# A two-layer perceiver kernel on one core: the second layer's context attention takes its value tiles as 128 keys by 512 columns, in halves, from a bank of their own

## Chip, core and metric

The kernel runs on one core of a Trainium2 chip. The metric is the device time of one execution in microseconds (us), the median of several. The engines are named as in the profile: PE is TensorE's matrix array, PEld its weight loads, DVE is VectorE, ACT is ScalarE, POOL is GpSimd, SP is SyncE, whose queue issues most transfers.

## What is computed

Two layers, each of a context attention, a self attention and a feed-forward part, over x of 8 batches by 128 rows by 512, with a context of 8 by 2048 keys by 512. All numbers are 4-byte floats. The change lies in the second layer's context attention and in the preparation for it:

```python
def _L1_xattn_ref(query, key, value, Wq, bq, Wk, bk, Wv, bv, Wo, bo):   # key = value = ctx_1024, 16 heads of 32
    ...
    q = query @ Wq.T + bq
    k = key @ Wk.T + bk
    v = value @ Wv.T + bv
    ...
    scores = jnp.einsum('bhtd,bhsd->bhts', q, k) * scale
    attn = jax.nn.softmax(scores, axis=-1)
    ctx = jnp.einsum('bhts,bhsd->bhtd', attn, v)
    return ctx @ Wo.T + bo
...
```

## The kernel before

The stages follow one another: the first layer's context attention ("swishmax"), its self attention ("twin"), the self attention of its feed-forward part ("plain"), the experts, then the second layer's context attention ("context", the function softmax_context), its kernel attention ("features") and the last nets. Within a stage each engine has an order of its own, written out by hand as a list of named tiles, and semaphores join them.

The context of a batch is four chunks of 512 keys. The heads are taken in four groups (slabs) of four heads, 128 columns of the weights each. A unit u is one batch b and one slab g (u = 4b + g, 32 in all); a step n is one unit and one chunk c (n = 4u + c). In step n TensorE makes, in the order of pe_step: the scores of (u, c) for four heads, the keys of (u+1, c), in chunk 0 the spread of the row maxima of u-1, in chunk 1 the sums of u-2, the transposed scores of (u-1, c), the values of the next unit, and "attend" of step n-5. VectorE takes the row maxima (L1426), the heads' quotient in chunk 1 (L1450 to L1454), the shift of the transposed scores (L1445) and the diagonal in chunk 3; ScalarE copies keys (L1405) and values (L1410) out of the banks and takes the exponentials (L1397); GpSimd adds them up (L1384 to L1387). The step's score needs the shifts of the step before, by head, since both use the same four banks; the transposed score needs this step's maxima.

The value product of the whole layer is v = context @ Wv. For 14 of the 32 chunks (the list AHEAD: chunks 0 and 2 of batches 0 to 6) it is made in earlier stages, 7 in twin, 5 in plain, 2 at the start of the experts (L1192, on the list "spare"), with all four slabs at once, as tiles of 128 keys by 512 columns; the result goes to DRAM (ahead.store) and the context stage loads it back by slab (load_values, L1345). The other 18 chunks are made in the context stage itself, L1555, one slab at a time: a tile of the step is 512 keys by 128 columns when chunk 0 of the batch is not in AHEAD, as for the last batch (16 products of 128 columns), and half of it (2 blocks of 128 keys, 8 products) in the other batches. Each f32 product is two instructions in the profile.

Beside these, once a batch: "norm", "hidden" (transposes of the normed rows, L1567) and "query" (L1573) for the next batch, "output" (L1579, then L1473 and L1474 on VectorE) for the batch before, and "later" (row statistics for the stage after; in the last batch but one also the reciprocal root for seven batches, L167 to L174, on VectorE). Their places in the unit are in pe_step and dve_step. All tiles but the scores and attend share a ring of three banks; a tile waits for the eviction of the tile three before it.

In the experts, SP's queue issues the loads of W1, then W2, then the stores of the chunks made ahead, then the first batch's context (four chunks) and the weights of keys and queries.

## Time and profile before

| | us |
|---|---|
| median of 3 runs | 4110.35 (4109.7 to 4110.72) |
| the profiled execution, its own time | 4110.32 |
| its span in the profile | 4108.5 |
| TensorE busy | 3995.8 (97%) |
| VectorE busy | 2177.3 (53%) |
| ScalarE busy | 1270.8 (31%) |
| GpSimd busy | 1003.8 (24%) |
| first product of the experts' part made ahead | at 2254.08 |
| first product of the context stage | at 2519.38 |
| step 0 of the context stage starts | at 2546.44 |
| first product of the stage after it | at 3820.17 |

A time such as 2519.38 is counted from the span's start. The granted clock (PEclk) is the share of full speed, 2.4 GHz, at which TensorE was let run: 1.00, or 0.50 when it is at 1.2 GHz. A busy row of TensorE overlaps the next by some 0.07 us, because products are pipelined; the distance of two starts is the better measure of what a tile takes.

### The profile page before, as it was taken

The numbers are of one execution on the slowest core, as the hardware profiler recorded it, in microseconds if no ns is written. First come the engines' busy times: TensorE is split into PE (matmuls) and PEld (weight loads), VectorE is DVE, ScalarE is ACT, GpSimd is POOL, SyncE is SP. The second block draws the span as 40 slices with busy tenths as digits, with TensorE's granted clock in tenths as the row PEclk, the third lists the DMA queues.
The fourth block names the chain that finished last, engine by engine and source line by source line (L and its number), as shares of the span: only waits on it lengthen the run. The fifth ranks groups of instructions, "written<-read, shape, count | busy, mean of one in ns | idle before, by whom it ended". The sixth has DMA issues, their size and how long they took to land. (4 is left out here: it accounts for less than half of the span.)

```text
span 4108.5 us, 73501 instructions
## 1 busy us (share of the span) xinstructions
PE 3995.8 (97%) x30656; PEld 2736.5 (67%) x30656; DVE 2177.3 (53%) x4381; ACT 1270.8 (31%) x3156; POOL 1003.8 (24%) x831
## 2 busy tenths in 40 slices
PE   8999999999999999899899999999999999998897
PEld 4777777777777778677465445666666666666675
DVE  5555555555555555255544324566665665546356
ACT  2222222222323222144233100333333333333344
POOL 2020202020202020022211000454454454445322
PEclk9999999999999999999999999999999999999899
DMA  4111111111111122211311400101101101101000
GB/s 144 62 62 62 62 62 62 62 62 62 62 61 63 58 66 73 88 29 35 108 42 48 163 0 29 55 24 45 58 24 45 58 25 45 50 1 45 11 2 21
DMA packets 127303, 219.86 MB, mean 54 GB/s; under 512 B 9088, under 2 KB 47616, under 8 KB 125184
## 3 DMA queue, kind: packets, MB, share of 16 engines
q1 hardware_dynamic: 118272, 181.60, 13.5%
q0 software_dynamic: 8704, 33.56, 2.5%
q8 instruction: 247, 4.05, 0.4%
q14 instruction: 80, 0.66, 0.1%
HBM read 198.35 MB, written 16.78 MB: 52 GB/s over the span
## 5 line engine op out<-in xcount | busy, mean ns | idle before, releaser
L577 PE MATMUL swishmax_attended<-swishmax_weights_t,swishmax_context 128*128 128x128 f32 x4096 | 520.1, 275 | 3.4 <-DVE swishmax_values_t L505 3.4
L1386 POOL TENSOR_TENSOR context_partial<-context_partial,context_weights_t 128x512 f32<-128x512 f32 x320 | 404.6, 1264 | 470.4 <-ACT context_weights_t L1397 452.7
L577 PEld LDWEIGHTS swishmax_attended<-swishmax_weights_t,swishmax_context 128*128 128x128 f32 x4096 | 487.9, 192 | 3.9 <-issue 3.9
L1546 PE MATMUL context_bank<-ahead_stream,ahead_staged 128*128 128x512 f32 x1024 | 473.3, 605 | 1.3 <-PEq L1072 1.3
L591 PE MATMUL swishmax_bank<-ahead_stream,ahead_w 128*128 128x512 f32 x1024 | 464.0, 596 | 7.2 <-DMA ahead_stream<-in_context_t_dram 7.2
L1445 DVE TENSOR_TENSOR context_weights_t<-context_score,context_shift 128x512 f32<-128x512 f32 x512 | 317.7, 683 | 231.9 <-PE context_score L1513 231.9
L435 ACT ACTIVATE swishmax_xes<-swishmax_score,swishmax_neg_max 128x512 f32<-128x512 f32 x256 | 177.2, 694 | 808.2 <-DVE swishmax_neg_max L470 808.2
L1426 DVE TENSOR_REDUCE context_neg_max<-context_score 128x1 f32<-128x512 f32 x512 | 317.9, 683 | 161.7 <-PE context_score L1498 161.4
L577 PE MATMUL swishmax_attended<-swishmax_weights_t,swishmax_sides 128*128 128x128 f32 x3072 | 384.9, 275 | 0.0
L1546 PEld LDWEIGHTS context_bank<-ahead_stream,ahead_staged 128*128 128x128 f32 x1024 | 184.0, 189 | 279.8 <-issue 272.2
L577 PEld LDWEIGHTS swishmax_attended<-swishmax_weights_t,swishmax_sides 128*128 128x128 f32 x3072 | 363.6, 192 | 0.0
L1397 ACT ACTIVATE context_weights_t<-context_weights_t 128x512 f32<-128x512 f32 x512 | 304.9, 629 | 181.8 <-DVE context_weights_t L1445 181.8
L591 PEld LDWEIGHTS swishmax_bank<-ahead_stream,ahead_w 128*128 128x128 f32 x1024 | 186.0, 192 | 198.8 <-issue 196.5
L409 POOL TENSOR_TENSOR swishmax_values_t<-swishmax_pair 128x256 f32<-128x256 f32 x32 | 23.4, 730 | 1172.3 <-ACT swishmax_pair L452 1172.2
L1405 ACT ACTIVATE context_keys_t<-context_bank,context_bias 128x512 f32<-128x512 f32 x128 | 88.0, 687 | 665.4 <-PE context_bank L1546 600.2
L1555 PE MATMUL context_bank<-ahead_w,ahead_stream 128*128 128x128 f32 x2304 | 290.4, 280 | 0.0
L1555 PEld LDWEIGHTS context_bank<-ahead_w,ahead_stream 128*128 128x128 f32 x2304 | 267.5, 192 | 18.3 <-issue 3.8
L470 DVE TENSOR_REDUCE swishmax_neg_max<-swishmax_score 128x1 f32<-128x512 f32 x256 | 164.7, 685 | 121.4 <-PE swishmax_score L562 121.4
L597 PEld LDWEIGHTS swishmax_bank<-whole_ident,swishmax_xes 128*128 128x128 f32 x1024 | 115.0, 141 | 163.7 <-issue 96.1
L475 DVE TENSOR_TENSOR swishmax_xes<-swishmax_xes,swishmax_score 128x512 f32<-128x512 f32 x256 | 175.5, 687 | 66.3 <-ACT swishmax_xes L435 66.3
L1513 PEld LDWEIGHTS context_score<-context_queries_t,context_keys_t 32*128 32x128 f32 x4096 | 132.6, 188 | 84.1 <-issue 69.9
L1387 POOL TENSOR_TENSOR context_partial<-context_partial,context_weights_t 128x512 f32<-128x512 f32 x128 | 164.3, 1284 | 10.0
(341 smaller groups left out, 5768.9 us busy)
## 6 DMA issues: line engine op xcount, KB each, us to landing
ahead_stream<-in_context_t_dram SPq DMA_DIRECT2D x78, 1024.0 KB, 5.8
swishmax_context<-in_context_dram POOLq DMA_DIRECT2D x32, 1024.0 KB, 5.9
swishmax_down<-_L_xattn_value_down_dram SPq DMA_DIRECT2D x64, 256.0 KB, 4.3
swishmax_up<-in_L_xattn_value_up_dram SPq DMA_DIRECT2D x32, 512.0 KB, 6.2
ahead_values<-ahead_staged SPq DMA_DIRECT2D x14, 1024.0 KB, 8.8
context_values<-ahead_values SPq DMA_DIRECT2D x56, 256.0 KB, 3.3
experts_w<-in_L_ffn_W_dram SPq DMA_DIRECT2D x16, 512.0 KB, 8.1
whole_x<-in_x_dram SPq DMA_DIRECT2D x8, 256.0 KB, 9.2
```

Source lines behind the costliest of these rows:

```text
L435: nc.scalar.activation(xes[:, n % XES, r, :], score[r][:], ACT.Exp, bias=neg_max[:, e, r, c:c + 1]).then_inc(exped, 1)
L470: nc.vector.tensor_reduce(neg_max[:, e, r, c:c + 1], score[r][:], AX.X, ALU.max, negate=True).then_inc(maxed, 1)
L475: nc.vector.tensor_tensor(xe, xe, score[r][:], ALU.mult).then_inc(weighted, 1)
L577: last = nc.tensor.matmul(product(i)[:, m, :], side(left, c, k, m), weights_t[:, n % 2, right, k, :], start=c == 0 and k == 0 and m == 0 a ...
L591: last = nc.tensor.matmul(bank_t[:], w_key[:, k, g * P:(g + 1) * P], context_t[:, c, k, :], start=k == 0, stop=k == DC - 1)
L1386: link(nc.gpsimd.tensor_tensor(acc, acc, w_t[:, :, k, :], ALU.add))
L1387: nc.gpsimd.tensor_tensor(acc, acc, w_t[:, :, DC - 1, :], ALU.add).then_inc(summed, 1)
L1397: nc.scalar.activation(weights_t[:, n % SLOTS, r], weights_t[:, n % SLOTS, r], ACT.Exp).then_inc(exped, 1)
L1426: nc.vector.tensor_reduce(neg_max[:, e, r, c:c + 1], score[r][:], AX.X, ALU.max, negate=True).then_inc(maxed, 1)
L1445: nc.vector.tensor_tensor(weights_t[:, n % SLOTS, r], score[r][:].rearrange("p (k q) -> p k q", q=P), shift[:, e, r, :].unsqueeze(1).broad ...
L1546: last = nc.tensor.matmul(bank_t[:], w["k"][:, k, g * P:(g + 1) * P], context_t[:, c, k, :], start=k == 0, stop=k == DC - 1)
L1555: last = nc.tensor.matmul(bank_t[:, i * P:(i + 1) * P], context_t[:, c, k, m * P:(m + 1) * P], w["v"][:, k, g * P:(g + 1) * P], start=k == ...
```

## The change

1. Chunks 0 and 2 of the last batch join AHEAD: 16 chunks ahead, 4 of them in the experts. There SP now issues, after W1, the load of the chunk two on and the store of each chunk, and W2 only then; the weights of keys and queries are put into the staging buffers of the last two chunks.
2. The 16 own chunks (1 and 3 of every batch) are made as tiles of 128 keys by all 512 columns (four products of 512 columns), one tile in two halves of two products, each half in a step of its own; two tiles of each batch are whole in one step, and two steps have none. They have a bank of their own ("value"), and each is copied once (L1410 before) into "made", three chunks deep; the chunks loaded from DRAM go to "fetched", six deep. Attend reads from one or the other.
3. The ring of the other tiles has two banks.
4. hidden moves from (g 2, c 1) to (g 1, c 3), query from (g 2, c 2) to (g 2, c 1), output from (g 1, c 2) to (g 2, c 0), later from (g 1, c 3) to (g 2, c 1).
5. The stage's opening has six halves between the four first keys; the feature stage's projection is loaded last. The load of a batch's context chunk now waits for the keys of that chunk only.

```diff
-AHEAD = [(b, c) for b in range(B) for c in (0, 2)][:14]
+AHEAD = [(b, c) for b in range(B) for c in (0, 2)]
 AHEAD_TWIN, AHEAD_PLAIN = 7, 5
...
+                for j in chunks:
+                    if j + 2 < len(AHEAD):
+                        sp.wait_ge(full_s, spare_ring.count(0, ("ahead", j, DC - 1)))
+                        ahead.load(sp, j + 2)
+                    sp.wait_ge(out_s, spare_ring.landed(0, ("ahead", j, DC - 1)))
+                    ahead.store(sp, j)
                 for e in range(E):
                     load(sp, w2[:, e], a["W2"][e], w2_loaded)
-                for j in chunks:
-                    sp.wait_ge(out_s, spare_ring.landed(0, ("ahead", j, DC - 1)))
-                    ahead.store(sp, j)
                 for c in range(NCH):
                     later.load_context_t(sp, 0, c)
-                for n, (name, j) in enumerate(zip("kq", chunks)):
+                for n, (name, j) in enumerate(zip("kq", chunks[-2:])):
                     sp.wait_ge(ahead.stored[j % 2], 16 * (j // 2 + 1))
                     load(sp, ahead.staged_weight(j % 2), later.dram[name], later.loaded[name])
...
-    KEYS, VALUES, SLOTS = 9, 12, 3
+    KEYS, FETCHED, MADE, SLOTS = 9, 6, 3, 3
...
-        values = s.sb("values", [P, VALUES, DC, P])
+        fetched = s.sb("fetched", [P, FETCHED, DC, P])
+        made = s.sb("made", [P, MADE, NG, DC, P])
...
-        bank = [s.ps(f"bank{n}", [P, CH]) for n in range(3)]
+        bank = [s.ps(f"bank{n}", [P, CH]) for n in range(2)]
+        value = s.ps("value", [P, CH])
...
-        value_landed = [s.sem(f"value_landed{n}") for n in range(4)]
+        value_full, value_out = s.sem("value_full"), s.sem("value_out")
+        value_landed = [s.sem(f"value_landed{n}") for n in range(2)]
...
-        def piece(u, c):
-
-            if (u, 0) in load_no:
-                return 1 + 2 * (c // 2), (2 * (c % 2), 2 * (c % 2) + 1)
-            return c, range(DC)
+        own_chunks = [(b, c) for b in range(B) for c in (1, 3)]
+
+
+        def made_slot(b, c):
+            return own_chunks.index((b, c)) % MADE
+
+        def value_tiles(n):
+
+            b, at = divmod(n + 6, 2 * NCH * 2)
+            if at < 12 and b < B:
+                return [("value", 2 * b, at // 2, at % 2)] if at < 8 else [("value", 2 * b + 1, (at - 8) // 2, at % 2)]
+            if at < 14 and b < B:
+                return [("value", 2 * b + 1, at - 10, h) for h in range(2)]
+            return []
 
         def pe_step(n):
             u, c = divmod(n, NCH)
             b, g = divmod(u, NG)
             out = [("score", u, c)] * (u < NU) + [("key", u + 1, c)] * (u + 1 < NU)
             out += [("sums", u - 2)] * (c == 1 and u >= 2) + [("spread", u - 1)] * (c == 0 and 1 <= u <= NU)
-            out += [("score_t", u - 1, c)] * (1 <= u <= NU) + [("value", u + 1, c)] * (u + 1 < NU)
+            out += [("score_t", u - 1, c)] * (1 <= u <= NU) + value_tiles(n)
             out += [("attend", (n - LAG) // NCH, (n - LAG) % NCH)] * (0 <= n - LAG < NU * NCH)
-            out += [("hidden", b + 1)] * (g == 2 and c == 1 and b + 1 < B) + [("query", b + 1)] * (g == 2 and c == 2 and b + 1 < B)
-            return out + [("output", b - 1)] * (g == 1 and c == 2 and b >= 1)
+            out += [("hidden", b + 1)] * (g == 1 and c == 3 and b + 1 < B) + [("query", b + 1)] * (g == 2 and c == 1 and b + 1 < B)
+            return out + [("output", b - 1)] * (g == 2 and c == 0 and b >= 1)
...
             out = [("key", u + 1, c)] * (u + 1 < NU) + [("spread", u - 1)] * (c == 0 and 1 <= u <= NU)
-            return out + exps[:2] + [("value", u + 1, c)] * (u + 1 < NU) + exps[2:]
+            return out + exps[:2] + [t for t in value_tiles(n) if t[3]] + exps[2:]
...
-            out += [("later", b - 1)] * (g == 1 and c == 3 and b >= 1)
-            out += [("hidden", b + 1)] * (g == 2 and c == 1 and b + 1 < B) + [("query", b + 1)] * (g == 2 and c == 2 and b + 1 < B)
-            return out + [("output", b - 1)] * (g == 1 and c == 2 and b >= 1)
+            out += [("later", b - 1)] * (g == 2 and c == 1 and b >= 1)
+            out += [("hidden", b + 1)] * (g == 1 and c == 3 and b + 1 < B) + [("query", b + 1)] * (g == 2 and c == 1 and b + 1 < B)
+            return out + [("output", b - 1)] * (g == 2 and c == 0 and b >= 1)
...
-        first_tiles = [(what, 0, c) for c in range(NCH) for what in ("key", "value")]
+        first_values = [[t for n in range(3 * k - 6, 3 * k - 3) for t in value_tiles(n)] for k in range(2)]
+        first_tiles = [("key", 0, 0), ("key", 0, 1)] + first_values[0] + [("key", 0, 2)] + first_values[1] + [("key", 0, 3)]
         pe_steps = first_tiles + [("hidden", 0), ("query", 0)] + [t for n in range(STEPS) for t in pe_step(n)] + [("output", B - 1)]
-        act_steps = first_tiles + [t for n in range(STEPS) for t in act_step(n)]
+        act_steps = [t for t in first_tiles if t[0] == "key" or t[3]] + [t for n in range(STEPS) for t in act_step(n)]
         dve_steps = [("norm", 0), ("hidden", 0), ("query", 0)]
         dve_steps += [t for n in range(STEPS) for t in dve_step(n)] + [("output", B - 1)]
-        ring = SharedRing(bank, [t for t in pe_steps if t[0] not in ("score", "score_t", "attend")],
+        ring = SharedRing(bank, [t for t in pe_steps if t[0] not in ("score", "score_t", "attend", "value")],
                           {"a": full_a, "d": full_d}, {"a": out_a, "d": out_d},
-                          lambda t: "a" if t[0] in ("key", "value", "spread") else "d")
+                          lambda t: "a" if t[0] in ("key", "spread") else "d")
...
                 def load_values(k):
                     u, c = from_dram[k]
-                    n = u * NCH + c
                     b, g = divmod(u, NG)
                     j = AHEAD.index((b, c))
                     sp.wait_ge(ahead.stored[j % 2], 16 * (j // 2 + 1))
-                    if k >= 4:
-                        sp.wait_ge(value_landed[k % 4], 16 * (k // 4))
-                    if n >= VALUES:
-
-                        sp.wait_ge(attended_chunk, n - VALUES + 1)
-                    sp.dma_start(values[:, n % VALUES].rearrange("p k d -> p (k d)"),
-                                 ahead.dram[j][:, g * D:(g + 1) * D]).then_inc(value_landed[k % 4], 16)
+                    if k >= 2:
+                        sp.wait_ge(value_landed[k % 2], 16 * (k // 2))
+                    if k >= FETCHED:
+
+                        before = from_dram[k - FETCHED]
+                        sp.wait_ge(attended_chunk, before[0] * NCH + before[1] + 1)
+                    sp.dma_start(fetched[:, k % FETCHED].rearrange("p k d -> p (k d)"),
+                                 ahead.dram[j][:, g * D:(g + 1) * D]).then_inc(value_landed[k % 2], 16)
 
                 def load_context(b, c):
 
-                    last = ("value" if (b * NG - 1, c) not in load_no else "key", b * NG - 1, c)
+                    last = ("key", b * NG - 1, c)
                     sp.wait_ge(ring.full_of(last), ring.count(last))
                     own.load_context_t(sp, b, c)
 
                 loads_at = {}
-                for k, (u, c) in enumerate(from_dram):
-                    loads_at.setdefault(max(-1, u * NCH + c - VALUES + LAG), []).append((load_values, k))
+                for k in range(len(from_dram)):
+                    u, c = from_dram[k - FETCHED] if k >= FETCHED else (-4, 0)
+                    loads_at.setdefault(max(-1, u * NCH + c + LAG), []).append(k)
                 for n in range(-1, NU * NCH):
-                    for load_one, k in loads_at.get(n, []):
-                        load_one(k)
+                    for k in loads_at.get(n, []):
+                        load_values(k)
                     b, c = divmod(n + 2 * NCH, NG * NCH)
                     if 1 <= b < B and c < NCH:
                         load_context(b, c)
+                sp.wait_ge(value_full, len(own_chunks) * DC)
                 for c, name in enumerate("qkvo"):
-                    last = ("value", NU - 1, c)
+                    last = ("key", NU - 1, c)
                     sp.wait_ge(ring.full_of(last), ring.count(last))
                     later.load(sp, name)
-                    if c == 0:
-
-                        last = ("value", NU - 1, NCH - 1)
-                        sp.wait_ge(ring.full_of(last), ring.count(last))
-                        later.load_proj(sp)
+                later.load_proj(sp)
 
             @block.gpsimd
             def _(pool):
@@ -1405,10 +1419,14 @@
                         nc.scalar.activation(keys_t[:, (u * NCH + t[2]) % KEYS, :], ring.bank(t)[:], ACT.Identity,
                                              bias=bias[:, 1, g:g + 1]).then_inc(out_a, 1)
                     elif what == "value":
-                        chunk, ms = piece(u, t[2])
-                        act.wait_ge(full_a, ring.count(t))
-                        nc.scalar.copy(values[:, (u * NCH + chunk) % VALUES, ms[0]:ms[-1] + 1],
-                                       ring.bank(t)[:, 0:len(ms) * P].rearrange("p (k d) -> p k d", d=P)).then_inc(out_a, 1)
+                        b, c = own_chunks[u]
+                        m = t[2]
+                        act.wait_ge(value_full, u * DC + m + 1)
+                        if u >= MADE:
+
+                            last = own_chunks[u - MADE]
+                            act.wait_ge(attended_chunk, (last[0] * NG + NG - 1) * NCH + last[1] + 1)
+                        nc.scalar.copy(made[:, made_slot(b, c), :, m, :], value[:].rearrange("p (g d) -> p g d", d=P)).then_inc(value_out, 1)
 
             @block.vector
             def _(dve):
@@ -1518,20 +1536,37 @@
                     if what == "attend":
                         c = t[2]
                         n = u * NCH + c
+                        b, g = divmod(u, NG)
                         if (u, c) in load_no:
                             k = load_no[(u, c)]
-                            pe.wait_ge(value_landed[k % 4], 16 * (k // 4 + 1))
+                            pe.wait_ge(value_landed[k % 2], 16 * (k // 2 + 1))
+                            values = fetched[:, k % FETCHED]
                         else:
-                            evicted(("value", u, c))
+                            pe.wait_ge(value_out, (own_chunks.index((b, c)) + 1) * DC)
+                            values = made[:, made_slot(b, c), g]
                         pe.wait_ge(exped, (n + 1) * HG)
                         if c == 0 and u:
                             pe.wait_ge(heads_out, u)
                         for k in range(DC):
                             for r in range(HG):
                                 cols = slice(r * HD, (r + 1) * HD)
-                                last = nc.tensor.matmul(attended[cols, :], values[:, n % VALUES, k, cols], weights_t[:, n % SLOTS, r, k, :],
+                                last = nc.tensor.matmul(attended[cols, :], values[:, k, cols], weights_t[:, n % SLOTS, r, k, :],
                                                         start=c == 0 and k == 0, stop=c == NCH - 1 and k == DC - 1)
                         last.then_inc(attended_chunk, 1)
+                        continue
+                    if what == "value":
+                        b, c = own_chunks[u]
+                        m, half = t[2], t[3]
+                        pe.wait_ge(w_loaded["v"], 16)
+                        pe.wait_ge(ctx_t_landed[c], 16 * (b + 1))
+                        if half == 0 and u * DC + m:
+
+                            pe.wait_ge(value_out, u * DC + m)
+                        for k in range(2 * half, 2 * half + 2):
+                            last = nc.tensor.matmul(value[:], context_t[:, c, k, m * P:(m + 1) * P], w["v"][:, k, :],
+                                                    start=k == 0, stop=k == DC - 1)
+                        if half:
+                            last.then_inc(value_full, 1)
                         continue
                     before = ring.before(t)
                     if before is not None:
@@ -1545,15 +1580,6 @@
                         for k in range(DC):
                             last = nc.tensor.matmul(bank_t[:], w["k"][:, k, g * P:(g + 1) * P], context_t[:, c, k, :],
                                                     start=k == 0, stop=k == DC - 1)
-                    elif what == "value":
-                        b, g = divmod(u, NG)
-                        c, ms = piece(u, t[2])
-                        pe.wait_ge(w_loaded["v"], 16)
-                        pe.wait_ge(ctx_t_landed[c], 16 * (b + 1))
-                        for i, m in enumerate(ms):
-                            for k in range(DC):
-                                last = nc.tensor.matmul(bank_t[:, i * P:(i + 1) * P], context_t[:, c, k, m * P:(m + 1) * P],
-                                                        w["v"][:, k, g * P:(g + 1) * P], start=k == 0, stop=k == DC - 1)
                     elif what == "spread":
                         pe.wait_ge(diagonal_set, u + 1)
                         last = nc.tensor.matmul(bank_t[:], ones[:], diagonal[:].rearrange("p r q -> p (r q)"), start=True, stop=True)
```

## Rows read from the trace of the kernel before

**Rows 1.** The page, part 1: busy us, share of the span, instructions.
```profile
PE 3995.8 (97%) x30656; PEld 2736.5 (67%) x30656; DVE 2177.3 (53%) x4381; ACT 1270.8 (31%) x3156; POOL 1003.8 (24%) x831
```

**Rows 2.** Busy time by stretch: experts' opening, context stage's opening, its tail.
```profile
core 0: us, PE busy (x) PEld busy (x) DVE busy (x) ACT busy (x) POOL busy (x), PEclk, DMA share, GB/s
2254.00:2282.00 28.00, 27.70 (x64) 12.08 (x64) 18.05 (x41) 4.28 (x8) 9.75 (x8) 1.00 0.97 359
...
2519.00:2546.40 27.40, 25.36 (x132) 17.34 (x132) 9.84 (x34) 4.13 (x8) 0.00 (x0) 1.00 0.35 106
...
3755.10:3820.20 65.10, 43.61 (x574) 28.86 (x572) 35.95 (x58) 19.97 (x33) 39.96 (x36) 0.76 0.11 41
```

**Rows 3.** Timeline, TensorE, one step (unit's second chunk): start, us busy, instruction.
```profile
2771.53 1.14 PE L1498 MATMUL context_score<-context_keys_t,context_queries_t 32*128 32x512 f32 x8
2772.60 3.70 PE L1546 MATMUL context_bank<-ahead_stream,ahead_staged 128*128 128x512 f32 x8
2776.23 0.43 PE L1563 MATMUL context_bank<-context_partial,context_ones 128*32 128x128 f32 x8
2776.58 1.17 PE L1513 MATMUL context_score<-context_queries_t,context_keys_t 32*128 32x128 f32 x32
2777.69 2.05 PE L1555 MATMUL context_bank<-ahead_w,ahead_stream 128*128 128x128 f32 x16
2779.67 1.08 PE L1532 MATMUL context_attended<-context_weights_t,context_values 128*32 128x128 f32 x32
```

**Rows 4.** Timeline, TensorE: keys and spread of a first chunk; last batch's value tile.
```profile
2762.94 3.70 PE L1546 MATMUL context_bank<-ahead_stream,ahead_staged 128*128 128x512 f32 x8
2766.48 1.02 PE L1559 MATMUL context_bank<-context_diagonal,context_ones 128*128 128x512 f32 x2
...
3578.40 3.84 PE L1555 MATMUL context_bank<-ahead_w,ahead_stream 128*128 128x128 f32 x32
```

**Rows 5.** Timeline, VectorE in the experts: idle time before its first gate copy.
```profile
2285.26 0.17 DVE L1144 COPY experts_gate<-experts_bank_d 128x8 f32<-128x8 f32 x1 [12.67 <-PE experts_bank_d L1209]
```

**Rows 6.** Timeline, the context stage's first keys and their copy.
```profile
2519.38 3.67 PE L1546 MATMUL context_bank<-ahead_stream,ahead_staged 128*128 128x512 f32 x8 [1.26 <-PEq L1072]
...
2525.51 0.69 ACT L1405 ACTIVATE context_keys_t<-context_bank,context_bias 128x512 f32<-128x512 f32 x1 [65.13 <-DMA context_bias_o<-in_L_xattn_bo_dram]
```

**Rows 7.** Timeline of a second chunk: its score, and VectorE's shifts behind the heads.
```profile
2848.76 1.14 PE L1498 MATMUL context_score<-context_keys_t,context_queries_t 32*128 32x512 f32 x8
...
2855.47 2.48 DVE L1445 TENSOR_TENSOR context_weights_t<-context_score,context_shift 128x512 f32<-128x512 f32 x4
```

**Rows 8.** Timeline, batch 0: a score held by the shifts of the step before.
```profile
2579.14 2.48 DVE L1445 TENSOR_TENSOR context_weights_t<-context_score,context_shift 128x512 f32<-128x512 f32 x4 [3.11 <-PE context_score L1513]
...
2581.03 1.77 PE L1498 MATMUL context_score<-context_keys_t,context_queries_t 32*128 32x512 f32 x8
```

**Rows 9.** Timeline, steps 119 and 120: first, one, and the end of "later"; the late transposed score.
```profile
3704.53 0.69 DVE L158 BATCH_NORM_STATS2 whole_features_stats<-whole_x 128x6 f32<-128x512 f32 x1
...
3707.15 1.20 DVE L174 SCALAR_TENSOR_TENSOR whole_features_rstd<-whole_features_tmp,whole_features_rstd 128x7 f32<-128x7 f32 x1
...
3709.95 2.48 DVE L1426 TENSOR_REDUCE context_neg_max<-context_score 128x1 f32<-128x512 f32 x4
...
3711.76 1.88 PE L1513 MATMUL context_score<-context_queries_t,context_keys_t 32*128 32x128 f32 x32
```

**Rows 10.** Timeline: the score of step 121, and the shifts of step 124.
```profile
3718.35 1.14 PE L1498 MATMUL context_score<-context_keys_t,context_queries_t 32*128 32x512 f32 x8
...
3755.14 2.48 DVE L1445 TENSOR_TENSOR context_weights_t<-context_score,context_shift 128x512 f32<-128x512 f32 x4 [1.04 <-PE context_score L1513]
```

**Rows 11.** SP's queue at a batch's second context chunk; the slowest landing (issue at 2627.42).
```profile
2780.87 0.32 SPq L1345 DMA_DIRECT2D context_values<-ahead_values  x1
2781.24 5.21 SPq L2069 DMA_DIRECT2D ahead_stream<-in_context_t_dram  x2
...
ahead_stream<-in_context_t_dram SPq DMA_DIRECT2D x1, 1024.0 KB, 6.9
```

## The prediction

> **What bounds the kernel now.** I read the page first: TensorE is busy 97% of the span, VectorE 53%, ScalarE 31% [rows 1]. Then the busy time by stretch: in the experts' opening, where the chunks made ahead fill TensorE, it has 27.70 us of work in 28 us. From 2519 on it is the context stage, where TensorE is full at the full clock until about 3750. From 3755.1 to 3820.2 it is busy 43.61 of 65.10 us at a mean granted clock of 0.76 of full speed: VectorE and GpSimd set the pace there, for no keys or values are left to make [rows 2]. So what the change does to TensorE's time counts in full up to about step 120 of the stage, and what it does to VectorE's queue counts after it.
>
> A step (one chunk of 512 keys for four heads) is, by the starts of TensorE's tiles [rows 3]: score 1.07, keys 3.63, sums 0.35, transposed score 1.11, half a unit's value tile 1.98, attend 1.01 us. The chunk that opens a unit has keys of 3.54 and a spread of 0.95, and a value tile of 16 products (32 instructions) takes 3.84 less the 0.07 by which a busy row overlaps the next, so 3.77 [rows 4]. The base without values is 6.82, plus 0.86 in a unit's first chunk and 0.35 in its second.
>
> **The price of a product.** Each 4-byte product is two instructions. Of 128 columns: 3.77 - 1.98 = 1.79 us for 16 instructions, 0.112 each. Of 512 columns: 27.70 / 64, about 0.43 each [rows 2], and keys of eight give 3.43 plus 0.2 us for the change of shape [rows 3]. Four narrow instructions (0.448) become one wide one (0.4285): 4% less, no more. Half a new tile (four wide instructions) is 1.71 + 0.20 = 1.91, a whole one 3.43 + 0.20 = 3.63.
>
> **Experts (added).** Two more chunks are 64 wide instructions: 27.4 us. Nothing hides them: before VectorE's first gate copy it has been idle 12.67 us, so the tokens that TensorE turns next were ready long since [rows 5]. The load of the 15th chunk goes out when the 13th is made (13.7 us in) behind 4 MB of W1. The loads of this stage move 359 KB per us [rows 2], so W1 ends some 12 us in and the chunk about 3 us after its issue; it is wanted at 27.4 us. The new order on SP's queue holds W2 back until the last chunk is stored, 55 us in. Its 4 MB need 12 us; the expert tiles start after 55 us more of inner tiles. No cost. **+27.4.**
>
> **Stage opening.** Four value tiles of 1.78 us (7.1) become six halves (10.3): +3.2. They now share one bank, so the first half of a second tile waits for ScalarE's copy of the one before: a copy of 0.59 (the copies of the chunks made ahead have this shape) and, as an estimate, 0.1 of signalling, twice: +1.4. ScalarE's first key copy waits for a bias until 2525.51, and the new second key tile ends after that [rows 6]. **+4.6.**
>
> **Steps 0 to 111.** A batch of 16 steps had 16 x 1.98 = 31.7 of values; now 12 halves and 2 whole tiles, 22.9 + 7.3 = 30.2: -1.5. The other tiles (hidden, query, output) only move. But VectorE is close behind: in a unit's second chunk its shifts begin 6.71 us after the score and last 2.48, to 9.19 [rows 7], and the next score needs them; a hold shows as a long score, 1.77 for 1.14, with keys 1.11 after the last shift [rows 8]. That step shrinks from 9.15 to 9.08, so three steps a batch lose about 0.07: batches 1 to 5 gain 1.4 each, **-6.8**. Batch 6 ends on four steps with the 3.77 tile, for the next batch was not ahead: -1.4 - 4 x 1.79, **-8.6**. In batch 0 step 8 has neither value nor output and lasts 7.68 against VectorE's 9.2: a hold of 1.6, and four opening tiles cost 1.88, not 1.98, before: **+0.6**.
>
> **Steps 112 to 120.** Nine tiles of 3.77 (33.9) become six halves and two whole ones (18.7): -15.2; a delay of 0.7 (1.88 for 1.17) and one of 0.2 behind batch 6's statistics go with them [rows 9]: **-15.9**. All this is repayment of work now done in the experts.
>
> **Steps 121 to 124.** Here a stall moves. Those statistics ("later", 16 small instructions at the last batch but one) occupy VectorE from 3704.53 to 3709.95, 5.4 us, one of them for 1.20 in place of 0.17 when GpSimd begins a sum [rows 9]. They stood in a step of 10.8 us with 3.77 of values behind it; now they stand in step 121, which is 7.17 us long (no value, no query), and the next two are 6.82. From the start s of step 121: shifts end at s+9.2, statistics at s+14.6 to 16; maxima 2.48 more; the shifts of step 122 start 1.04 later (the row at 3755.14 shows the 1.04 [rows 10]) at s+18.1 to 19.5 and end 2.4 later. Step 123's score and keys end 1.11 + 3.63 later, the shifts start 1.2 after, at s+26.4 to 27.9, and end, with the diagonal, at s+29.8 to 31.2. Step 124's maxima and shifts then put its first shift at s+33.3 to 34.8. Before, it is 3755.14 - 3718.35 = 36.8 [rows 10]. So these steps, which shed three tiles (11.3 us), give back only 2.0 to 3.5: **-2.7**. The rest, about 8.5 us, is the new wait. The Trainium skill (SBUF — State Buffer, "Who interferes with whom") says a VectorE instruction with two SBUF inputs blocks for a whole GpSimd instruction that reads SBUF; that 1.20 us row agrees. By that rule, with GpSimd summing throughout, the statistics would be nearer 7 us than 5.4 and the step -2.0; the middle I take stands without it.
>
> **The clock.** TensorE stands idle or waiting some 2 us in step 122 and 3 to 4 more before its transposed score. The tail before shows the clock at half after such waits (mean 0.76 over the last 65 us [rows 2]). If the keys of step 123 (3.63) fall on half clock, that costs up to 3.6; none if not. I take **+1.5**.
>
> **Other edits.** The second context chunk of a batch is now wanted by the value tile of the step after its load, not three steps on. Its issue is about 0.5 us after an attend (it goes out behind a value load that waits for the same attend [rows 11]); the query tile (3.8) and 5.8 us of score, keys and transposed score come first, so it has 9.1 us and the slowest took 6.9 [rows 11]. No cost. Two ring banks in place of three: each tile's forerunner by two is evicted at least one long tile earlier. The value copies stay one per tile, 0.59, on an engine that is idle more than half of a step. The loads from DRAM keep a lead of 12 steps. The feature weights' projection goes out last, 60 us before use.
>
> **Sum:** 27.4 + 4.6 + 0.6 - 6.8 - 8.6 - 15.9 - 2.7 + 1.5 = +0.1 us. With the profile's own 4110.32 (span 4108.5 and 1.8 around it; the median of the runs is 4110.35, so no correction) that is 4110.4; since the small holds that I left out (a step's 0.35 us margin between VectorE and the next score) can only add, I take **4111 us**.
>
> **Rivals.**
> *A: the tail does not stall so, and the tile is what it seems.* If the statistics slip between the steps (VectorE had margin I did not see) or overlap the missing keys, 8.5 us of wait shrink to about 1 and the clock stays up: 4111 - 7.5 - 1.5 = 4102. For it: VectorE is busy only 53% of the span. Against it: the order on VectorE is fixed, and the row of 1.88 shows the same statistics already delaying a longer step. Beyond it, a cheaper opening: 4100. Chance 0.15.
> *B: VectorE becomes the pace of ordinary steps.* Each step is 0.07 shorter, with 0.35 us left between the last shift (8.4 after the score in a middle chunk) and the next score (8.73). If the shift comes later by more than 0.35 us, because score and transposed score wait on maxima that the moved output and statistics delay, each of some 100 steps loses what exceeds it; at 0.1 us that is +10: 4121. For it: one row in four already shows a hold. Against: the holds of before are 0.07 each. Chance 0.09.
> *C: the context chunk lands late.* It decides from 9.1 us after issue; at 11 us it would cost 1.9 in each of seven batches, +13: 4124. The landings of 5.4 to 6.9 speak against it. Chance 0.03.
> *D: the clock stays at half through the tail.* The Trainium skill (TensorE: Matmul & The Clock Gate, "HAM oscillation — how this bites in real kernels") warns that idle gaps between bursts throttle the array again and again; the rows show half clock in the tail, none before 3755. In rows' terms: 3.6 for step 123's keys, 1.3 for its score and attend, and as much again if the short tiles of steps 124 to 127 (some 8 us of TensorE's time) run at half: +8 over the forecast, 4119. Chance 0.05.
> *Main: all as summed,* within 0.2%: 0.68.
>
> **Numbers.** 0.2% is 8.2 us, about what a measurement of this kernel can tell from no change. Inside the main case's own bounds (opening 3.2 to 4.6, tail -3.5 to 0, clock 0 to 3.6) the time is 4107 to 4116. The range reaches to A and most of B and D: 4102 to 4119. Faster by over 0.2% (below 4102.1): A's better part, 0.12. Slower (above 4118.6): most of B, C and D, 0.15. Same: 0.73.
>
> **What the changed profile would show.** In the experts, 128 wide instructions in 55 us and a first token tile at about 2310. In the steps, four wide value instructions with the attend 1.91 after them, and a batch period near 152.5. Step 121's score and the first shift of step 124 33 to 35 us apart, with TensorE waiting for VectorE's maxima after the statistics, some 25 us before the key-less steps' pace of before sets in. Wrong would be a value half held behind a landing or a value copy, a batch period above 154, or no wait at step 122.

## The result and the profile after

The changed kernel takes **4120.25 us**, the median of 11 runs (4116.32 to 4122.03), against 4109.81 us of the kernel before (11 runs, 4104.71 to 4111.81). The ratio is 1.0027, interval 1.0017 to 1.0036. So it is slower, by a quarter of a per cent: about 10 us where 1 was forecast, and 1 us above the upper end of the range. The profiled execution took 4116.32 us (span 4114.5), the fastest of its eleven, and the profile of before 4110.32. Those two differ by 6.0 us, and the rows below explain these 6; the remaining 4 are taken up with the experiments.

Busy time by stretch of the changed kernel: experts' opening, context stage's opening, batch 1 (steps 16 to 31), steps 121 to 124, tail. The first, second and last stand for [rows 2].

```profile
core 0: us, PE busy (x) PEld busy (x) DVE busy (x) ACT busy (x) POOL busy (x), PEclk, DMA share, GB/s
2253.30:2308.90 55.60, 55.15 (x128) 24.18 (x128) 17.92 (x41) 9.21 (x16) 9.62 (x8) 1.00 0.56 192
2546.00:2578.20 32.20, 28.99 (x92) 14.53 (x92) 9.70 (x34) 4.50 (x7) 0.00 (x0) 1.00 0.30 91
2718.10:2871.50 153.40, 152.68 (x1436) 75.85 (x1432) 93.40 (x156) 55.26 (x93) 76.18 (x60) 1.00 0.14 42
3725.50:3761.50 36.00, 31.48 (x291) 16.97 (x290) 28.84 (x51) 9.92 (x16) 16.34 (x13) 0.95 0.30 96
3761.50:3826.10 64.60, 44.50 (x572) 29.24 (x571) 35.70 (x58) 19.97 (x33) 40.29 (x36) 0.74 0.00 1
```

The page: TensorE has 1,728 instructions fewer, yet only 3.5 us less work than in [rows 1].

```profile
PE 3992.3 (97%) x28928; PEld 2576.7 (63%) x28928; DVE 2181.2 (53%) x4381; ACT 1269.8 (31%) x3100; POOL 1003.9 (24%) x831
...
L1566 PE MATMUL context_value<-ahead_w,ahead_stream 128*128 128x512 f32 x512 | 248.4, 613 | 1.5 <-ACT context_made L1429 1.5
```

TensorE should be full in the third stretch, and it is idle for 0.7 of 153.40 us. The timeline of two steps of batch 1 shows where (start, us, instruction, in brackets the idle time before it; the last row is cut short by the end of the view). The first step answers to [rows 3] in place (a unit's second chunk), but is the one with the query tile:

```profile
2806.02 1.14 PE L1516 MATMUL context_score<-context_keys_t,context_queries_t 32*128 32x512 f32 x8
2807.09 3.70 PE L1581 MATMUL context_bank<-ahead_stream,ahead_staged 128*128 128x512 f32 x8
2810.72 0.43 PE L1589 MATMUL context_bank<-context_partial,context_ones 128*32 128x128 f32 x8
2811.07 1.17 PE L1531 MATMUL context_score<-context_queries_t,context_keys_t 32*128 32x128 f32 x32
2812.97 1.08 PE L1553 MATMUL context_attended<-context_weights_t,context_fetched 128*32 128x128 f32 x32 [0.72 <-DVE context_heads_t L1472]
2813.98 3.84 PE L1599 MATMUL context_bank<-context_hidden_t,ahead_staged 128*128 128x128 f32 x32
2817.74 1.14 PE L1516 MATMUL context_score<-context_keys_t,context_queries_t 32*128 32x512 f32 x8
...
2823.55 1.98 PE L1566 MATMUL context_value<-ahead_w,ahead_stream 128*128 128x512 f32 x4
2825.46 0.75 PE L1553 MATMUL context_attended<-context_weights_t,context_made 128*32 128x128 f32 x20
```

The reader is to see three things. A half of four wide instructions takes 1.91 us to the next row, as forecast. The query tile takes 3.76. And the attend of the first step comes 1.90 after the transposed score in place of 1.11: it stood idle for VectorE's heads. This wait was in no term of the sum. The waits of all attend tiles put it together, for the changed kernel:

```profile
  issue: 88.6, 114
  DVE context_heads_t L1472: 7.5, 10
```

In the kernel before, the same view shows 2.9 us in 2 times behind the heads. (The "issue" line belongs to the weight loads of the same tiles, PEld, which has little to do under a half of wide products; asked for PE alone, the view doesn't have that line.)

The tail, steps 121 to 123 (timeline, without the weight loads), which answers to [rows 9, 10]:

```profile
3725.49 1.14 PE L1516 MATMUL context_score<-context_keys_t,context_queries_t 32*128 32x512 f32 x8
...
3734.61 0.68 DVE L158 BATCH_NORM_STATS2 whole_features_stats<-whole_x 128x6 f32<-128x512 f32 x1
...
3735.54 1.25 DVE L167 TENSOR_SCALAR whole_features_var<-whole_features_mv 128x7 f32<-128x7 f32 x1
...
3736.90 1.24 DVE L169 TENSOR_SCALAR whole_features_tmp<-whole_features_var 128x7 uint32<-128x7 uint32 x1
...
3739.73 1.12 DVE L174 SCALAR_TENSOR_TENSOR whole_features_rstd<-whole_features_tmp,whole_features_rstd 128x7 f32<-128x7 f32 x1
...
3742.08 2.48 DVE L1444 TENSOR_REDUCE context_neg_max<-context_score 128x1 f32<-128x512 f32 x4
3742.83 3.86 PE L1531 MATMUL context_score<-context_queries_t,context_keys_t 32*128 32x128 f32 x32 [3.33 <-DVE context_neg_max L1444]
...
3761.46 2.48 DVE L1463 TENSOR_TENSOR context_weights_t<-context_score,context_shift 128x512 f32<-128x512 f32 x4 [1.04 <-PE context_score L1531]
```

The statistics lie ahead of step 122's maxima, as forecast, but take 7.5 us (3734.61 to 3742.08). TensorE waits 3.33 for the first of the four maxima (one a head), and then its transposed score takes 3.86 in place of 1.17. Two things are in that row. Its products need the maxima head by head, and the last of these ends at 3744.56, 1.7 after the row's start. And from 3744.5 to 3747.9 the granted clock is at half (busy time by stretch, this kernel):

```profile
3742.80:3744.40 1.60, 1.34 (x6) 0.88 (x6) 1.60 (x3) 0.00 (x0) 0.00 (x0) 1.00 0.71 271
3744.50:3747.90 3.40, 3.29 (x51) 2.96 (x54) 1.65 (x4) 0.85 (x2) 0.00 (x0) 0.50 0.00 0
```

What the row takes when it follows the maxima so with the clock at 0.99 stands in the tail of the second experiment's kernel:

```profile
3771.32 2.94 PE L1532 MATMUL context_score<-context_queries_t,context_keys_t 32*128 32x128 f32 x32 [0.41 <-DVE context_neg_max L1445]
```

So some 1.8 us of the row are the maxima and 0.9 the clock.

### The profile page after: what moved, and what is told of

Same layout as the page of the kernel before. It is cut to its first block and busy times, and to the rows that moved or that the text cites. A ratio compares the mean times of both kernels' runs of the same rounds, so it can differ in the third digit from the quotient of the medians.

```text
span 4114.5 us, 70074 instructions
## 1 busy us (share of the span) xinstructions
PE 3992.3 (97%) x28928; PEld 2576.7 (63%) x28928; DVE 2181.2 (53%) x4381; ACT 1269.8 (31%) x3100; POOL 1003.9 (24%) x831
## 5 line engine op out<-in xcount | busy, mean ns | idle before, releaser
L1566 PE MATMUL context_value<-ahead_w,ahead_stream 128*128 128x512 f32 x512 | 248.4, 613 | 1.5 <-ACT context_made L1429 1.5
L1531 PE MATMUL context_score<-context_queries_t,context_keys_t 32*128 32x128 f32 x4096 | 161.6, 288 | 4.9 <-DVE context_neg_max L1444 3.7
```

What stands on the lines that cost most here:

```text
L1531: last = nc.tensor.matmul(score[r][:, k * P:(k + 1) * P], keys_t[rows, n % KEYS, k * P:(k + 1) * P], queries_t[rows, b % 2, g, :], start=T ...
L1566: last = nc.tensor.matmul(value[:], context_t[:, c, k, m * P:(m + 1) * P], w["v"][:, k, :], start=k == 0, stop=k == DC - 1)
```

## The experiments

Each was timed beside the kernel before, whose median was 4109.6 to 4110.1 in every group (22 to 33 runs). "Own time" is that of a profiled execution.

| kernel | median, us | ratio to before, interval | own time |
|---|---|---|---|
| changed kernel, again | 4118.97 | 1.0022 [1.0012, 1.0031] | 4120.09 |
| statistics finished late | 4112.82 | 1.0007 [0.9997, 1.0016] | 4115.24 |
| query tile ahead of attend | 4112.44 | 1.0008 [0.9999, 1.0017] | 4112.44 |
| both | 4107.33 | 0.9995 [0.9986, 1.0005] | 4105.17 |
| kernel before, again | 4110.09 | 1.0 [0.9991, 1.0009] | 4107.4 |
| old tiles, sixteen ahead | 4116.51 | 1.0016 [1.0007, 1.0025] | 4115.27 |
| the same, statistics late | 4110.99 | 1.0004 [0.9994, 1.0013] | 4107.66 |
| both, old order on SP's queue | 4123.03 | 1.0029 [1.0016, 1.0041] | 4121.05 |
| kernel before, mended | 4106.56 | 0.9994 [0.9985, 1.0003] | 4108.31 |
| both, and sums ahead of keys | **4102.89** | **0.9985 [0.9976, 0.9994]** | 4100.63 |

**The changed kernel again.**

> The changed kernel once more, for its spread and a second profile. Its median was 10 us above the kernel before, the one execution profiled only 6.0 (span 4114.5 against 4108.5). Theory 1 (the waits are fixed, the rest is the clock): the same step starts to within 0.1 us up to step 121, batch period 153.3, and wherever this execution is longer than 4114.5 TensorE shows more time at half clock, in the tail or behind it: 8 us more of half clock for 4 us more time. Rival: the extra 4 us are waits of VectorE or a transfer in the ordinary steps, then the step starts themselves drift apart before step 121. Time 4118 to 4122.

The loss repeats: +9.1 us in the medians. Its profile is 3.8 us longer than the first one's, and it is already 6.0 longer before the changed stages begin: the experts' opening starts at 2259.27 in place of 2253.28. Busy time by stretch, in the same early stretch of work, of this run:

```profile
1648.00:1693.00 45.00, 38.94 (x280) 34.46 (x281) 12.49 (x32) 1.76 (x3) 0.72 (x1) 0.88 0.00 1
```

and of the first profile of the changed kernel:

```profile
1646.00:1687.00 41.00, 34.99 (x281) 31.94 (x281) 12.51 (x31) 1.76 (x3) 0.72 (x1) 1.00 0.00 1
```

The same instructions take 4 us more where the granted clock is 0.88 of full speed. So the longer time is clock, as the first theory had it, but in the first stages and not in the tail, and single profiles of one kernel differ by some 4 us.

**The statistics' finish moved out of steps 121 and 122**, to stand before the last heads; in the step only their first two instructions are left:

```diff
+        dve_steps.insert(dve_steps.index(("heads", NU - 1)), ("finish", B - 2))
...
-                        if u == B - 2:
-                            later.rows.finish(nc, link, range(B - 1))
+                    elif what == "finish":
+                        later.rows.finish(nc, link, range(B - 1))
```

> The 13 small VectorE instructions of the reciprocal root for seven batches move from step 121 to just before the last heads, where VectorE idles 10 us for GpSimd's sums. Theory 1 (they hold up steps 122 to 124 and bring the clock down): steps 121 to the first shift of 124 fall from 36.0 to about 30 us, the half-clock stretch near 3744 is gone, and the time falls by 6 to 9 us against the changed kernel. Rival (VectorE bounds these key-only steps anyway, by maxima and shifts): the stretch falls to 34 at best and the time by 0 to 2 us.

It gives back 6.2 us in the median. From the start of step 121 to the first shift of step 124 it takes 30.24 us (3728.90 to 3759.14), as expected. Timeline of this kernel:

```profile
3736.86 2.41 PE L1517 MATMUL context_score<-context_keys_t,context_queries_t 32*128 32x512 f32 x8
...
3738.94 2.48 DVE L1445 TENSOR_REDUCE context_neg_max<-context_score 128x1 f32<-128x512 f32 x4
...
3744.94 2.73 PE L1517 MATMUL context_score<-context_keys_t,context_queries_t 32*128 32x512 f32 x8
...
3814.18 0.96 DVE L1469 RECIPROCAL context_inverse<-context_bank 128x128 f32<-128x128 f32 x1 [2.24 <-PE context_bank L1590]
```

Step 122 lasts 8.08 us (3736.86 to 3744.94) where the changed kernel's lasts 14.77 (3733.45 to 3748.22). At its new place the finish costs nothing: the reciprocal of the last heads still waits 2.24 for its sums.

**The query tile ahead of the attend**, and the context load ahead of the value loads on SP's queue, since the tile delays the attend that a value load waits for:

```diff
+            out += [("query", b + 1)] * (g == 2 and c == 1 and b + 1 < B)
             out += [("attend", (n - LAG) // NCH, (n - LAG) % NCH)] * (0 <= n - LAG < NU * NCH)
...
-                    for k in loads_at.get(n, []):
-                        load_values(k)
                     b, c = divmod(n + 2 * NCH, NG * NCH)
                     if 1 <= b < B and c < NCH:
                         load_context(b, c)
+                    for k in loads_at.get(n, []):
+                        load_values(k)
```

> In the step of (slab 2, chunk 1) the query tile goes ahead of attend on TensorE, and SP issues the next batch's context chunk before the value load that waits for that attend. Theory 1 (attend opens a new unit there and waits 0.79 us for the heads' quotient, since no value tile lies in between): the gap before attend is gone in seven batches, batch period 153.3 to 152.5, time 5 to 6 us less than the changed kernel. Rival (VectorE paces the steps and takes the gain back as a longer score in the step after): period stays at 153.2 or more, 0 to 1 us.

It gives back 6.5 us. The wait is gone, here in batch 1:

```profile
2813.73 1.17 PE L1532 MATMUL context_score<-context_queries_t,context_keys_t 32*128 32x128 f32 x32
2814.83 3.84 PE L1600 MATMUL context_bank<-context_hidden_t,ahead_staged 128*128 128x128 f32 x32
2818.60 1.08 PE L1554 MATMUL context_attended<-context_weights_t,context_fetched 128*32 128x128 f32 x32
2819.61 1.14 PE L1517 MATMUL context_score<-context_keys_t,context_queries_t 32*128 32x512 f32 x8
```

and attend tiles wait for the heads 1.7 us in 3 times, not 7.5 in 10. A batch takes 152.55 in place of 153.34 (starts of steps 16 and 32: 2720.80 and 2873.35; changed kernel 2718.14 and 2871.48). The queue's new order was not run alone on the changed kernel; there no value half waits for a context chunk (TensorE's waits before its value tiles are 1.5 us in 2 times, all for ScalarE's copy in the opening), so there was no wait that it could have removed.

**Both edits together.**

> The two edits of the runs before together. If they are separate waits, their gains add: 11 to 15 us below the changed kernel, 4105 to 4109, so 1 to 4 us below the kernel before. If both merely hand the wait on to VectorE, the sum is under 5 us and it stays above 4115.

11.6 us less than the changed kernel, of 12.7 if the two added up: separate causes. With both mended the new tiles are 2.6 us under the kernel before, an interval that still takes in no change.

**The kernel before, again.**

> The kernel before once more, as a control for the first stages. The changed kernel's second profile and those of its three variants reach the start of the twin stage 5 us later than the profiles of before and of the changed kernel shown with the result (1691.8 to 1693.0 against 1686.9 and 1687.4), with the same instructions up to there and half clock at 1648 and for 10.2 us at 1685. Theory 1 (a chance state of the clock that any of these kernels can have): some executions of the kernel before show it too, and its times spread by some 5 us. Rival (it comes with the change, through where its data lies): this profile starts twin at 1687 again and the median stays at 4110.

The median stays, and its eleven times spread from 4104.45 to 4112.6. The question that it was run for has an answer: the kernel before shows the dip of the clock too. It reaches the twin stage at 1690.73, not at 1687.41, with half clock on the way:

```profile
1646.00:1690.70 44.70, 38.45 (x280) 33.97 (x281) 12.67 (x32) 1.76 (x3) 0.72 (x1) 0.88 0.00 1
```

The kernel before, mended (below), does so too, at 1691.70. So the dip doesn't come with the change. As a whole this profile is 2.9 us shorter than the first one of before, with the context stage and tail together shorter: the first profile of before was a somewhat long one there (experts' opening to the features' first product: 1566.1 and 1561.3 us). The same stretch of the changed kernel takes 1572.8 and 1571.5. Two profiles of each therefore differ by 8.5 on average, near the 9 to 10 of the medians.

**Old tiles, sixteen chunks ahead.** The kernel before, with only this:

```diff
-AHEAD = [(b, c) for b in range(B) for c in (0, 2)][:14]
+AHEAD = [(b, c) for b in range(B) for c in (0, 2)]
```

and the experts' loads and stores in the changed order.

> The kernel before with one part of the change alone: all 16 chunks ahead, the experts' loads and stores in the new order; values in the context stage stay 512 keys by 128 columns, statistics and query stay where they were. Theory 1: 27.4 us added in the experts, 16 tiles of 3.77 become 1.98 (-28.6), the late transposed scores at steps 119 and 120 (0.9) give way to about 2.7 us of waiting for the statistics, now in a step of 8.8 us: within 1 us of before, plus at most 2 for the clock; 4109 to 4113. Rival (the longer experts' part has a cost of its own, in its loads or its clock): 4115 or more.

4116.51 is over what was expected. This half alone costs 6.4 us against the kernel before, again, and the timeline shows the statistics again, at their old place in step 120:

```profile
3714.35 1.14 PE L1501 MATMUL context_score<-context_keys_t,context_queries_t 32*128 32x512 f32 x8
3714.64 0.69 DVE L158 BATCH_NORM_STATS2 whole_features_stats<-whole_x 128x6 f32<-128x512 f32 x1
...
3721.59 2.48 DVE L1429 TENSOR_REDUCE context_neg_max<-context_score 128x1 f32<-128x512 f32 x4
3722.34 3.86 PE L1516 MATMUL context_score<-context_queries_t,context_keys_t 32*128 32x128 f32 x32 [2.36 <-DVE context_neg_max L1429]
...
3730.59 1.14 PE L1501 MATMUL context_score<-context_keys_t,context_queries_t 32*128 32x512 f32 x8
```

Step 120 lasts 16.24 us, not 9.66. In the kernel before, the steps of the last batch have a value tile of 3.77 us each, here of 1.98; with the longer ones the statistics began 1.7 us before step 120, and here 0.3 after its start, among GpSimd's sums. There they cost 0.7 (the late transposed score of [rows 9]), here 6.6: a wait of 2.36, a transposed score of 3.86, and a value tile of 3.52 for 2.05. So the stall doesn't need the new tiles: shorter value tiles in the last steps are enough.

**The same with the statistics finished late** (the edit of the second experiment).

> The run with 16 chunks ahead and the old tiles, and the statistics of seven batches moved behind the last shifts. That run's trace lost 6.6 us in step 120 (16.24 us for 9.66 of tiles): VectorE's statistics, four of their small instructions held to 1.1 or 1.2 us by GpSimd's sums, and then half clock on the value tile (3.52 us for 2.05). Theory 1 (moving the work ahead costs nothing by itself; the statistics had been hidden by the long tiles that it took away): the step is 9.7 again and the time falls 6 to 8 us to the kernel before's, 4109 to 4111. Rival (the cost is in the experts or the clock there): it stays above 4114.

5.5 us back, step 120 at 9.66 (3710.05 to 3719.71), and the two more chunks ahead are free but for 0.9 us, within what can be told from nothing: the 27.4 us paid are repaid.

**Both edits, with SP's queue in the order of the change** (value loads ahead of the context load).

> The two edits together, but SP's queue in the change's order: the value load that waits for attend is ahead of the context chunk's load. Theory 1: attend now ends after the query tile, so the chunk's load has 5.8 us before the value tile wants it and takes 5.3 to 6.4 after the 0.5 to its issue: TensorE waits 0.5 to 1.5 us before a value tile in seven batches, and the time is 4 to 9 us above the run with both edits and the new queue order, 4111 to 4116. Rival (the load is hidden in any case): as that run, 4107.

It is dearer than expected: 15.7 us over the kernel with both, with six runs only, and these spread from 4113.98 to 4125.92. TensorE, timeline:

```profile
2977.20 1.17 PE L1533 MATMUL context_score<-context_queries_t,context_keys_t 32*128 32x128 f32 x32
2980.83 3.58 PE L1568 MATMUL context_value<-ahead_w,ahead_stream 128*128 128x512 f32 x4 [2.46 <-issue]
```

and SP's queue, two rows of its timeline (x2: two issues):

```profile
2972.68 0.32 SPq L1363 DMA_DIRECT2D context_fetched<-ahead_values  x1
2973.06 4.63 SPq L2097 DMA_DIRECT2D ahead_stream<-in_context_t_dram  x2
```

The context load goes out behind the value load at 2973.06, against 2965.68 with the load first, and a value half that wants it at 2978.4 starts at 2980.83, 7.8 after the issue (the landings of this stretch took up to 7.7). The half itself then takes 3.58 for 1.98, at a granted clock of half speed (busy time by stretch):

```profile
2980.70:2984.10 3.40, 3.27 (x4) 1.18 (x4) 0.17 (x1) 0.84 (x2) 2.34 (x2) 0.50 0.35 131
```

From step 32 to 96 a batch takes 155.1 in place of 152.55. In the seven batches this half waits 0.83 to 2.46 us, 10.2 in all; after the two longest waits, 2.46 and 2.41, it takes 3.58 and 3.65, after the others 1.96.

**The kernel before, mended**: the old tiles with fourteen ahead, the statistics late, and the sums ahead of the keys in every unit's second chunk:

```diff
-            out = [("score", u, c)] * (u < NU) + [("key", u + 1, c)] * (u + 1 < NU)
-            out += [("sums", u - 2)] * (c == 1 and u >= 2) + [("spread", u - 1)] * (c == 0 and 1 <= u <= NU)
+            out = [("score", u, c)] * (u < NU) + [("sums", u - 2)] * (c == 1 and u >= 2) + [("key", u + 1, c)] * (u + 1 < NU)
+            out += [("spread", u - 1)] * (c == 0 and 1 <= u <= NU)
```

> The kernel before with the statistics moved to the end and the sums tile ahead of the keys in every unit's second chunk, so that heads are ready before the shifts. Theory 1 (the four holds of 0.07 a batch and 0.9 at steps 119 and 120 go): 3 us less than before, 4106 to 4108. Rival (VectorE's place in the step does not matter there, TensorE is full): within 1 us of before.

3.5 us in the median, with an interval that just takes in no change; a batch takes 153.60, not 153.82.

**Both edits, and the sums ahead of the keys** in the second chunks of three units out of four (the fourth has the long query tile):

```diff
+            early = c == 1 and u >= 2 and g != 2
+            out = [("score", u, c)] * (u < NU) + [("sums", u - 2)] * early + [("key", u + 1, c)] * (u + 1 < NU)
+            out += [("sums", u - 2)] * (c == 1 and u >= 2 and not early) + [("spread", u - 1)] * (c == 0 and 1 <= u <= NU)
```

> The changed kernel with both edits (4107.33 in its own comparison), and the sums tile ahead of the keys in the second chunk of slabs 0, 1 and 3, so that VectorE's heads are done before its shifts. Theory 1: the three holds of 0.14 a batch go, the batch period falls from 152.5 to 152.1, 3 us less: 4103 to 4105, some 5 us below the kernel before. Rival (holds are noise of the busy rows, or keys wait for the bank in their turn): 4107 or more.

**4102.89 us**, 4.4 under the kernel with both and 0.15% under the kernel before, with the whole interval below 1. A batch takes 152.13. Against the kernel before, mended, which was run in the same group, the new tiles with sixteen chunks ahead are 3.7 us faster. TensorE has no idle time left in the stretch that had 0.7:

```profile
2718.00:2871.40 153.40, 153.40 (x1465) 76.25 (x1464) 94.58 (x159) 56.77 (x95) 76.19 (x60) 1.00 0.13 42
```

## Why the prediction was wrong

By its own steps, profile against profile:

| step | forecast | measured |
|---|---|---|
| experts | +27.4 | +27.4 |
| stage opening | +4.6 | +5.2 |
| batch 0 | +0.6 | +1.0 |
| batches 1 to 5 | -6.8 | -2.4 |
| batch 6 | -8.6 | -7.6 |
| steps 112 to 120 | -15.9 | -15.8 |
| steps 121 to 124, with the clock | -1.2 | -0.8 |
| rest of the tail, and before the experts | 0 | -1.1 |
| sum (measured: of unrounded terms) | +0.1 | +6.0 |

**The step that failed** is "The other tiles (hidden, query, output) only move". Where they move from matters. The attend of the step where a unit's weights are first used starts a new sum in its bank, and waits until VectorE has read the last one, the heads:

```
                            pe.wait_ge(heads_out, u)
```

The heads wait for the sums tile, which in that step stands behind 3.63 us of keys. In [rows 3] a half value tile stands between the transposed score and the attend and covers the wait, and in three units of four it still does. The change takes it from the fourth and puts the query tile behind the attend. That is 0.79 us in each of seven batches, 5.5 in all (an eighth wait, in step 121, costs nothing: the next score is held by VectorE's shifts, which end at 3734.69). The batch period is 153.34 against 152.5 forecast: of the 153.82 before, the values take 1.48 off, and this wait puts 0.79 back and three longer holds 0.21. The experiment isolates the wait: 0.79 a batch, 6.5 in the median. Of the 5.9 us by which batches 0 to 6 came out above their forecast, it is 5.5; the rest lies in the holds, of which the sum took 0.12 a batch.

**Mis-sized terms.** The tail's mechanism was right: the statistics, the place, the maxima that wait. Its size was not: 7.5 us in place of 5.4, because four small instructions on 7 values a row took 1.1 to 1.25 us each while GpSimd summed, each ending within 0.04 us of the end of one of GpSimd's four. (They are 15 instructions, not 16.) In the kernel before the last part of the same chain had two, of 1.20 [rows 9] and 1.12, because there GpSimd's sums began at 3707.07, with four of the chain left; the forecast kept their cost though the place had changed. The prediction named the rule of the Trainium skill (SBUF — State Buffer, "Who interferes with whom") and that by it the statistics would be nearer 7; the 7.5 is nearer to that, and the middle value I took was wrong. Two of the four held rows (L172, L174) have two SBUF inputs, as the rule wants; L167 and L169 have one and a constant, and were held as long. Steps 121 to 124 then took 35.97 us to the first shift, against 33.3 to 34.8 forecast and 36.8 before: 1.3 more than the middle by the statistics, and 0.7 by the clock (step 122's shifts start 1.75 after the maxima, not 1.04). The clock's +1.5 was taken for the keys of step 123; what ran at half was the end of step 122's transposed score and its attend, about 0.9 and 0.6, of which only the 0.7 holds VectorE. So that the sum of these steps came out near the forecast (-0.8 against -1.2) is luck: the statistics were taken too low and the clock too high. The opening: both halves that were to wait did, for 0.77 us and not 0.69, and the rest is in its other tiles. Timeline of the changed kernel:

```profile
2552.96 3.60 PE L1566 MATMUL context_value<-ahead_w,ahead_stream 128*128 128x512 f32 x8
2557.32 1.96 PE L1566 MATMUL context_value<-ahead_w,ahead_stream 128*128 128x512 f32 x4 [0.77 <-ACT context_made L1429]
```

**What held.** The price of an instruction (128 wide ones in 55.15 us, 0.43 each), no cost for the delayed W2, the repayment of steps 112 to 120 to 0.1 us, and that the wide tiles shed 1.5 us a batch (153.60 of the kernel before, mended, against 152.13 of the fastest, which differ in a batch by little else).

**The rivals.** A (no stall in the tail) was wrong as a forecast, but the late finish builds what it described and is worth 6.2 us. B (VectorE sets the pace) was right in kind and small in size: in three steps of a batch, each behind a unit's second chunk, the score is held 0.14 us in place of 0.07 (1.21 to the next start, and 1.14 before, where an unheld one has 1.07), and the sums ahead of the keys took 0.42 off a batch, three times 0.14. C (a late context chunk) didn't occur, but with a lead shortened by one query tile it did, at 7.8 us from the issue: it was nearer than its chance said, and the changed kernel's slowest landing took 7.6 of the 9.1. D (a long half clock in the tail): the last 64.6 us had a mean of 0.74 against 0.76, so little of it.

**The median against the profile.** The two shown profiles differ by 6.0 us and the medians by 10.4 (9.1 in the repetition). The known causes, measured as medians, are 11.6; the tiles with both mended are 2.6 under before. The remaining difference is how the two first profiles fell. Both were short in the early stage (the twin stage starts at 1687.41 and 1686.93, in the ten later profiles at 1690.73 to 1693.02), but that of before was long in its last stages, which made up for it. The dip of the clock before the twin stage stands in all ten later profiles, those of the kernel before and of its mended form among them, so it doesn't need the change; why it is in neither first profile was not isolated. Wide tiles with only fourteen chunks ahead were not tried either.

## What to carry to other kernels

When a tile moves out of a slot, look for the wait behind that slot, not only at the tile's own cost: filler between a producer and its consumer is a cover, and moving it can cost on every turn of the loop what it saved. Work that repays itself (chunks made ahead) also removes the cover at the far end, so list what small work of another engine lived under it and move that first; a few tiny instructions beside another engine's large ones can cost several microseconds. Where edits are worth a few tenths of a per cent, compare medians over many runs, and take the terms from more than one profile of each kernel.

## What the hardware showed

- Four VectorE instructions on 128x7 values took 1.11 to 1.25 us beside GpSimd's sums (3.98 us for three, then more), where the others of the chain took 0.17; each of the four ended within 0.04 us of the end of one GpSimd instruction. At the late place (3803.26 to 3811.94) six of them were held so, the chain took 8.7 us, and TensorE did not wait for it.
- With TensorE full before and after, a value half took 3.58 and 3.65 us for 1.98 behind waits of 2.46 and 2.41, at a granted clock of 0.50; behind five waits of 0.83 to 1.44 in the same place it took 1.96. Each of these two waits thus cost some 1.6 more than its own length. Behind a wait of 3.33 the clock was at 0.50 from 3744.5 to 3747.9.
- A row of 32 narrow instructions that takes 1.17 us took 2.94 at a clock of 0.99 when it followed VectorE's four maxima, and 3.86 with half clock on top: a long row is not all clock.
- The same early stage took 41 or 45 us, at a mean granted clock of 1.00 or 0.88, in kernels whose instructions there are the same, and 44.7 at 0.88 in the kernel before too.
